# Two small-head attentions on one core: a new order of the steps on TensorE, and the output products moved into the token job

## The reference

```
x  = L0_attn_x                       # (16, 256, 128)
xn = layernorm(x)
s  = windowed attention(xn)          # 16 heads of 8, window 64, a bias by distance
g  = silu(mixture of 8 experts(xn))
x  = x + s * g
xn = layernorm(x)
s  = full attention(xn)              # 16 heads of 8, biases on q, k, v, out, a bias by position
g  = silu(two inner transformer layers(xn))
x  = x + s * g
```

## Time and profile before

| | |
|---|---|
| median of 3 runs | 2148.72 us (2146.99 to 2150.23) |
| the profiled execution's own time | 2146.38 us |
| its span | 2144.6 us |
| busy: PE, PEld, DVE, ACT, POOL | 1690.7, 1161.8, 1470.2, 1217.2, 1105.0 us |
| windowed attention | about 104 to 341 us |
| full attention | about 744 to 1135 us |
| inner layers and end | about 1140 to 2144 us |

### The profile page before, as it was taken

The page is one execution under the profiler, slowest core; times in us unless marked ns, Lnnn a source line. Parts: engine busy times, 40 slices in busy tenths (PEclk is TensorE's granted clock), DMA queues, the critical chain, the costliest instruction groups (busy, mean ns, idle before and its releaser), DMA issues. The chain is left out here.

```text
span 2144.6 us, 47031 instructions
## 1 busy us (share of the span) xinstructions
PE 1690.7 (79%) x18545; PEld 1161.8 (54%) x18545; DVE 1470.2 (69%) x1945; ACT 1217.2 (57%) x2068; POOL 1105.0 (52%) x599
## 2 busy tenths in 40 slices
PE   1399996999994489999993578787787887778873
PEld 1266664666662167776771355555555555555552
DVE  3488884444456099999993677777777777777733
ACT  0167764444442167777772467666666666676643
POOL 0176662444442066776673655555555555555503
PEclk9999998999997689999996799999999999999995
DMA  3100000000000200000002010000000000000101
GB/s 94 44 3 2 3 3 13 12 7 6 12 0 6 83 2 2 2 2 3 2 2 69 13 23 21 21 21 18 20 21 20 16 19 21 21 21 19 23 19 39
DMA packets 52350, 40.18 MB, mean 19 GB/s; under 512 B 24424, under 2 KB 44172, under 8 KB 52020
## 3 DMA queue, kind: packets, MB, share of 16 engines
q1 hardware_dynamic: 52148, 37.35, 6.8%
HBM read 15.75 MB, written 2.13 MB: 8 GB/s over the span
## 5 line engine op out<-in xcount | busy, mean ns | idle before, releaser
L438 POOL TENSOR_TENSOR a_prob<-a_prob,a_top 128x1024 f32<-128x1024 f32 x192 | 359.7, 1894 | 132.7 <-DVE a_top L651 132.7
L645 DVE TENSOR_TENSOR a_prob<-ps,a_table 128x1024 f32<-128x1024 f32 x192 | 226.2, 1220 | 109.9 <-PE ps L505 54.7
L1117 POOL TENSOR_TENSOR i_qk<-i_raw,i_rot 128x1024 f32<-128x1024 f32 x64 | 176.2, 2753 | 214.0 <-ACT i_raw L1324 214.0
L1476 DVE TENSOR_TENSOR i_rt<-i_raw,i_rot 128x512 f32<-128x512 f32 x128 | 239.2, 1911 | 61.4 <-ACT i_raw L1324 58.4
L612 ACT ACTIVATE a_probT<-ps 128x1024 f32<-128x1024 f32 x192 | 196.2, 1022 | 89.0 <-PE ps L515 89.0
L877 POOL TENSOR_TENSOR e_hh<-e_h,e_hh 128x512 fp32r<-128x512 f32 x112 | 144.2, 1290 | 195.1 <-ACT e_hh L864 193.4
L651 DVE TENSOR_REDUCE a_top<-a_prob 128x4 f32<-128x1024 f32 (+1 forms) x192 | 225.2, 1215 | 9.1 <-issue 0.4
L607 ACT ACTIVATE a_prob<-a_prob 128x1024 f32<-128x1024 f32 x192 | 202.3, 1054 | 32.8 <-POOL a_prob L438 32.8
L515 PEld LDWEIGHTS ps<-ident,a_prob 128*128 128x128 f32 x1536 | 167.0, 141 | 95.1 <-issue 59.3
L515 PE MATMUL ps<-ident,a_prob 128*128 128x128 f32 x1536 | 207.8, 279 | 8.4 <-ACT a_probT L612 3.4
L1324 ACT ACTIVATE i_raw<-ps 128x1024 f32<-128x1024 f32 x64 | 65.5, 1024 | 215.6 <-PE ps L1164 215.5
(11 more groups left out here) (199 smaller groups left out, 3686.3 us busy)
## 6 DMA issues: line engine op xcount, KB each, us to landing
i_V<-i_V SPq DMA_DIRECT2D x96, 130.0 KB, 2.3
a_prob<-skew_scratch SPq DMA_DIRECT2D x2, 2048.0 KB, 9.3
X<-in_L_attn_x SPq DMA_DIRECT2D x4, 512.0 KB, 5.8
a_table<-in_c_l_table SPq DMA_DIRECT2D x1, 2048.0 KB, 7.6
e_xs<-Y SPq DMA_DIRECT2D x8, 256.0 KB, 2.3
i_ms<-Y SPq DMA_DIRECT2D x16, 128.0 KB
out_dram<-X SPq DMA_DIRECT2D x4, 512.0 KB, 3.3
i_ms<-Y SPq DMA_DIRECT2D x16, 127.0 KB
```

What stands on the lines that cost most here:

```text
L438: nc.gpsimd.tensor_tensor(s, s, top[:, slot].unsqueeze(2).broadcast_to([P, HG, KW]), ALU.subtract).then_inc(shifted, 1)
L645: nc.vector.tensor_tensor(prob[:, slot].rearrange("p (b x) k -> p b x k", b=2), ps[:, 2 * (n % 2):2 * (n % 2) + 2, :].rearrange("p b (x k) ...
L1117: nc.gpsimd.tensor_tensor(s, raw[:, T % 2], cosines, ALU.mult).then_inc(cos_done, 1)
L1476: last = nc.vector.tensor_tensor(rt[:, j].rearrange("p h (s d) -> p h s d", s=2), src, table.unsqueeze(1).broadcast_to([P, FH, 2, HF]), AL ...
```

## The change

It does four things in both attentions.

1. The order within a step on TensorE becomes scores, auxiliary jobs, transpositions, sums (before: jobs, scores, transpositions, sums, y). On ScalarE a job now comes behind the exponential of its step, no longer ahead of it.
2. The y jobs are gone. The token job, now `xy`, in the place of x (step iU-7), holds the transpositions for sequence i and the output products of both tiles of sequence i-DELAY (4 windowed, 3 full), the latter in the upper half of bank 7. `oT` has 4 slots in place of 2.
3. One copy of 256 columns writes `S` for both tiles. In the windowed attention ScalarE copies `xT` and then `S`. In the full one, from sequence 3 on, both are done by VectorE, as `tensor_copy` and `tensor_tensor`, in the step of the job and behind `normalise`; only the second of them frees the bank. For the first three sequences ScalarE still copies `xT`.
4. `LAST` grows, so that the xy jobs of the last sequences have a step (step 69 windowed, 137 full).

No transfer and no instruction of GpSimd is added, taken away or put elsewhere in its queue.

```
-        AT = {"x": -7, "qk": -6, "v": 0} if windowed else {"x": -7, "qk": -6, "v": -3}
+        AT = {"xy": -7, "qk": -6, "v": 0} if windowed else {"xy": -7, "qk": -6, "v": -3}
+        DELAY = 4 if windowed else 3
+        LAST = (NBATCH + DELAY - 1) * U + AT["xy"] + 1
...
 TensorE, job:
-                if kind == "x":
-                    for k in range(TPB):
-                        last = nc.tensor.transpose(ps[:, 7, k * P:(k + 1) * P], Y[:, i * TPB + k, :], ident[:, :])
+                if kind == "xy":
+                    if i < NBATCH:
+                        for k in range(TPB):
+                            last = nc.tensor.transpose(ps[:, 7, k * P:(k + 1) * P], Y[:, i * TPB + k, :], ident[:, :])
+                    if i >= DELAY:
+                        for k in range(TPB):
+                            T = (i - DELAY) * TPB + k
+                            pe.wait_ge(o_sb, T + 1)
+                            last = nc.tensor.matmul(ps[:, 7, (2 + k) * P:(3 + k) * P], oT[:, T % 4, :], wT[:, 3, :],
+                                                    start=True, stop=True)
...
-                    pe.wait_ge(o_sb, T + 1)
-                    last = nc.tensor.matmul(ps[:, 7, 0:P], oT[:, T % 2, :], wT[:, 3, :], start=True, stop=True)
 TensorE, steps:
             for step in range(FIRST, LAST):
-                for n, kind, i, tile in jobs_at(step, 0):
-                    job(n, kind, i, tile)
                 if step % 2 == 0 and 0 <= step + AHEAD < UNITS:
                     score(step + AHEAD)
+                for n, kind, i in jobs_at(step):
+                    job(n, kind, i)
                 if 0 <= step < UNITS:
                     transposes(step)
                 if 0 <= step - 2 < UNITS:
                     sums((step - 2) // 2, step % 2)
-                for n, kind, i, tile in jobs_at(step, 1):
-                    job(n, kind, i, tile)
 ScalarE, steps:
             for step in range(FIRST, LAST):
-                for n, kind, i, tile in jobs_at(step, 0):
-                    if windowed or kind != "v":
-                        job(n, kind, i, tile)
                 if 0 <= step + 1 < UNITS:
                     exp(step + 1)
+                for n, kind, i in jobs_at(step):
+                    if windowed or kind == "qk" or (kind == "xy" and i < DELAY):
+                        job(n, kind, i)
                 if 0 <= step < UNITS:
                     keep_probT(step)
 VectorE, job:
+                elif kind == "xy":
+                    if i < NBATCH:
+                        last = nc.vector.tensor_copy(xT[:, i % 2, PAD:PAD + SEQ], ps[:, 7, 0:SEQ])
+                    at = (i - DELAY) * TPB
+                    last = nc.vector.tensor_tensor(S[:, at:at + TPB, :], ps[:, 7, SEQ:2 * SEQ].rearrange("p (k e) -> p k e", e=P),
+                                                   bvo[:, 1:2, :].broadcast_to([P, TPB, P]), ALU.add)
+                last.then_inc(aux_free, 1)
 VectorE, steps:
                 if r == 0 and 1 <= T <= TILES:
                     normalise(T - 1)
...
                 if step % 2 == 0 and 0 <= n < UNITS:
                     add_bias(n, n % NBUF)
                     add_bias(n + 1, (n + 1) % NBUF)
+                for a, kind, i in jobs_at(step):
+                    if not windowed and (kind == "v" or (kind == "xy" and i >= DELAY)):
+                        job(a, kind, i)
                 dve.drain()
```

More of the change, by code:

```diff
@@ L352, in head_attention, with jobs_at, job_of @@
         NZERO = 5 + (2 if windowed else 0)
-        AT = {"x": -7, "qk": -6, "v": 0} if windowed else {"x": -7, "qk": -6, "v": -3}
[L355 to L366, removed]
+        AT = {"xy": -7, "qk": -6, "v": 0} if windowed else {"xy": -7, "qk": -6, "v": -3}
+        FIRST = AT["xy"]
+        DELAY = 4 if windowed else 3
+        LAST = (NBATCH + DELAY - 1) * U + AT["xy"] + 1
+        JOBS = sorted([(i * U + AT[kind], kind, i) for i in range(NBATCH) for kind in AT]
+                      + [(i * U + AT["xy"], "xy", i) for i in range(NBATCH, NBATCH + DELAY)])
+        def jobs_at(step):
+            return [(n, kind, i) for n, (s, kind, i) in enumerate(JOBS) if s == step]
+        def job_of(kind, i):
+            return [j[1:] for j in JOBS].index((kind, i)) + 1
         def unit(n):
@@ L465, in _, with job @@
             pe.wait_ge(zeroed, NZERO)
-            def job(n, kind, i, tile):
+            def job(n, kind, i):
                 after(pe, aux_free, n)
                 par = i % 2
-                if kind == "x":
-                    for k in range(TPB):
-                        last = nc.tensor.transpose(ps[:, 7, k * P:(k + 1) * P], Y[:, i * TPB + k, :], ident[:, :])
+                if kind == "xy":
[8 more added lines that the diff above has]
+                                                    start=True, stop=True)
                 elif kind == "qk":
@@ L577, in _, with job @@
                 act.wait_ge(bq_scaled, 1)
-            def job(n, kind, i, tile):
+            def job(n, kind, i):
                 act.wait_ge(aux_ps, n + 1)
                 par = i % 2
-                if kind == "x":
-                    nc.scalar.activation(xT[:, par, PAD:PAD + SEQ], ps[:, 7, 0:SEQ], ACT.Copy).then_inc(aux_free, 1)
+                if kind == "xy":
+                    if i < NBATCH:
+                        last = nc.scalar.activation(xT[:, par, PAD:PAD + SEQ], ps[:, 7, 0:SEQ], ACT.Copy)
+                    if i >= DELAY and windowed:
+                        at = (i - DELAY) * TPB
+                        last = nc.scalar.activation(S[:, at:at + TPB, :], ps[:, 7, SEQ:2 * SEQ].rearrange("p (k e) -> p k e", e=P),
+                                                    ACT.Copy)
+                    last.then_inc(aux_free, 1)
                 elif kind == "qk":
@@ L592, in job @@
                         nc.scalar.activation(qT[:, par, :], q, ACT.Identity, bias=bqk[:, 2:3], scale=SCALE).then_inc(aux_free, 1)
[L593 to L600, removed]
-                else:
-                    nc.scalar.activation(S[:, i * TPB + tile, :], ps[:, 7, 0:P], ACT.Copy).then_inc(aux_free, 1)
+                else:
+                    for v in range(NVT):
+                        for k in range(TPB):
+                            src = ps[:, 7, (v * TPB + k) * P:(v * TPB + k + 1) * P]
+                            last = nc.scalar.activation(V[:, par, v, k, :, :, 0:D],
+                                                        src.rearrange("p (g x d) -> p g x d", g=4, x=QG), ACT.Copy)
+                    last.then_inc(aux_free, 1)
             def exp(n):
@@ L615, in _ @@
             for step in range(FIRST, LAST):
-                for n, kind, i, tile in jobs_at(step, 0):
-                    if windowed or kind != "v":
-                        job(n, kind, i, tile)
                 if 0 <= step + 1 < UNITS:
                     exp(step + 1)
+                for n, kind, i in jobs_at(step):
+                    if windowed or kind == "qk" or (kind == "xy" and i < DELAY):
+                        job(n, kind, i)
                 if 0 <= step < UNITS:
                     keep_probT(step)
-                if windowed:
-                    for n, kind, i, tile in jobs_at(step, 1):
-                        job(n, kind, i, tile)
         @block.vector
```

25 lines of the change are left out of this document (10 added, 15 removed).

## The result

The changed kernel takes 2169.18 us (median of 4 runs, 2168.68 to 2173.89), the kernel before 2147.85 us beside it. The ratio is 1.0104 (1.0086 to 1.0121): 21.3 us slower. The profiled execution has a span of 2167.3 us against 2144.6. The forecast was 2163 and slower.

A forecast was written before the change was run, and what follows sets the result against it. TensorE's queue was taken as the bound, VectorE close behind. Full attention loses 34.4 us, windowed gains 20.4: 14.0 on 2148.7 gives 2162.7, forecast 2163 us (2154 to 2172; 8 in 10: 2143 to 2176).

The forecast's parts named there:

- Windowed attention, 13.04 us for a sequence: Windowed sequence falls from 14.50: two y removed (1.70), output matmuls added (0.49), qk and v cheaper (0.14, 0.11).
- rival 4: Windowed attention: saving is small because xy makes waits; half of 20.4 us lost, 2173 us; chance 0.08.
- Wait A: Full attention, from sequence 3: qk waits 1.74 us for VectorE's copies behind normalise to free the bank.
- Wait B: Full attention, every sequence: transpositions of step 4 wait 1.28 us for the chain through kM, shift, exp and copy.
- rival 1: Full attention: Wait B doesn't come, 1.3 us x 15 less, 2143.5 us; chance 0.09.
- rival 2: Full attention: Wait A doesn't come, as VectorE catches up; 22.6 us less, 2140 us; chance 0.06.
- rival 3: Full attention: neither wait comes and it stays unchanged; the whole gains 20.4 us, 2128 us; chance 0.06.
- rival 6: Waits are smaller than counted, each by half a microsecond: 2150 us; chance 0.08.
- TensorE's work, 23.03: Full-attention sequence: 23.52 us less two y of 0.42, plus 0.49 for output matmuls, less 0.14 for qk.
- 13 sequences at +2.53, 32.9: Full attention, sequences 3 to 15: each takes 26.05 us, 2.53 more than before, adding 32.9 us.
- rival 5: Full attention: TensorE's clock falls; at 0.93, 1.7 us more a sequence, 23 in all, 2185 us; chance 0.08.
- Sequences 0 to 2 and the tail of the full attention, 1.5: Sequences 1 and 2, with Wait B alone, add about 1 us; the tail with wider copies adds 0.5.

The follow-up runs named there:

- e10: e3 with all xT copies on ScalarE and, in steps up to 0, jobs ahead of scores and of exp as before the change: 2122.5 us.
- e1: Changed kernel with VectorE's xy copies of the full attention, from sequence 3, put ahead of normalise in their step: 2148.2 us.
- e2: Changed kernel with mask_keys (kM) of the full attention one unit later in GpSimd's queue: 2165.7 us.
- e3: Changed kernel with the edits of both e1 and e2: 2130.0 us, 0.9922 of the kernel before.
- e6: Changed kernel with the old order, jobs ahead of scores on TensorE and ahead of exp on ScalarE, keeping xy jobs and merged copies: 2191.1 us.
- e9: Changed kernel with one more VectorE copy of 256 columns from bank 7 into a spare tile, ahead of the xT copy: 2177.0 us.
- e8: e2 with scores issued twice into the same banks ahead of each qk of full-attention sequences 3 to 15: 2152.0 us.

## Why the forecast held, and where it was off

- **Windowed attention, 13.04 us for a sequence.** Measured 12.94 to 12.95. The wait at y went as priced (0.85 us each), and no new wait came, so rival 4 falls. The Trainium skill's Perfetto Trace Analysis, section Matmuls, asks for independent groups to rotate through banks. The trace agrees where a copy stands between two jobs of one bank with nothing else to do (y before, qk in the full attention after), and the windowed stage shows that one bank is enough where other work stands between. The start was taken as unchanged and cost 4.7 us (third token job 22.2 us after the first, 17.5 before), of which the rest of the stage gave back 1.2 beyond the forecast. This step was missing: the forecast walked the steady state and added nothing for the start, where scores and qk wait for each other's engines. e10 shows it to be the order.
- **Wait A, 1.74.** Counted from start to start, as the forecast did, it is 905.29-902.32-1.07 = 1.90. The 0.16 more is VectorE's lag: `normalise` starts 903.07-901.31 = 1.76 after the sums of its step, 1.61 in the forecast. e1 shows that it comes of the place of the copies behind `normalise`. The copy of `xT` takes 0.42 us for 256 columns and the add 0.41, as put down (0.76 for the two; from 904.48 to 905.23 it is 0.75). The Trainium skill's VectorE: DVE Perf Modes, section Why PSUM operands drop a tier, holds a float32 operand from PSUM to the single rate. The trace agrees: the copy is no cheaper than the add.
- **Wait B, 1.28.** 912.81-910.44-1.07 = 1.30. e2's sequences of 25.00 and e3 show it. So rivals 1, 2 and 3, each with a wait that doesn't come, fall, and so does rival 6: both waits are a little longer than counted, not shorter.
- **TensorE's work, 23.03.** 26.16-1.90-1.30 = 22.96. Qk ahead of transpositions costs 906.26-905.29 = 0.97, 0.09 less than before and not 0.14. With that, the four output matmuls and the rest are within 0.1 of what was put down.
- **13 sequences at +2.53, 32.9.** Measured 35.3 (from the token job at 794.46 to that at 1135.44 us, against 13 x 23.515): 26.23 on average. One sequence of 26.5 us has a wait A longer by 0.37. In one of 26.7 the granted clock fell, behind the qk at 852.44 (stretches of 851 to 857.5 and to 873):

```profile
851.00:857.50 6.50, 5.06 (x49) 4.10 (x50) 5.92 (x8) 1.86 (x3) 2.82 (x2) 0.74 0.00 0
...
857.50:873.00 15.50, 15.08 (x254) 10.68 (x256) 11.94 (x13) 11.24 (x12) 12.23 (x8) 1.00 0.01 2
```

- **The clock, rival 5, chance 0.08.** It had the clock and the wrong size: 23 us if the whole stage ran at 0.93. Here the granted clock fell in single stretches, once in twelve sequences of the changed kernel, where it cost 0.5 us (wait B shrank to 0.31 beside it), and in 8 of 12 of e2's. It decided what e2, e6 and e9 took.
- **Sequences 0 to 2 and the tail of the full attention, 1.5.** Measured 5.6: 3.4 up to the third token job (45.2 us after the first, against 41.8), 0.3 in the next sequence (as forecast), and 1.9 in the tail, where the last xy job waits 1.96 us for VectorE to finish `normalise` and the copy of the job ahead. Of the 3.4, some 2.6 are the longer stretch at the lower clock, by what separates e2 and e8; the 0.8 left is near the 0.7 of the forecast for that sequence (1.28-0.14-0.42). So this part of the miss is chance, or something that these runs don't show, and the tail is the part that the forecast sized too small.

So the term that was mis-sized is the one for what is not steady: 4.7 us at the windowed start, for which the forecast had nothing, and 5.6 at the start and end of the full attention, for which it had 1.5; 2.6 of the 5.6 went with the clock there and not with the order. The stretch between the stages gave 1.6 back; nothing of the change is in it.

## What to carry to other kernels

When one bank serves as a slot for small jobs, ask on which engine's queue its copy is written, and behind what: a copy of 0.4 us behind an instruction that waits for the end of TensorE's own step costs TensorE the whole detour. Measure a chain's slack from the trace before moving what starts it; 0.35 us of slack against a move of 1.07 and a removal of 0.42 gave the second wait to within 0.05 us. Price the start and the tail with the same walk as the steady state. Before a gain in one stage of one profile is laid to an edit, look for a kernel with the same code in that stage: here e8 showed 2.6 us that e10's edit had not brought.

## What the runs showed of the hardware

Removing a wait can be worth nothing if another idle stretch lowers TensorE's clock. e2 waits 1.23 us less in each sequence than the changed kernel at wait B, and 8 of its 12 sequences are 1.4 to 2.1 us longer than the others, with 3.4 us at a granted clock of 0.50; filling 1.07 us of the idle time with repeated matmuls (e8) made the sequences and the tail together 13.3 us shorter (the whole kernel 13.7). These are the idle stretches ahead of qk, once in a sequence, and the sequences of twelve with a fall of the clock: up to 0.77 us (e1), 0.93 (e3) and 1.47 (e8), none; 1.82 (changed kernel), one; 1.97 (e2), eight; 2.15 (e9), eight; 3.04 (e6), all, and each sequence of e6 is at least 1.7 us longer than work and waits make it. Single waits of 2.19 us in the changed kernel, 2.33 in e2 (at 930.6 us) and 2.52 in e9 (at 855.4 us) had no fall behind them, so the length of the wait alone doesn't settle it. What else does, these runs don't show.
